# A three-layer transformer block in two stages: keys and values side by side, other PSUM banks, a stacked last chunk, gather first

## The reference

```
x = x + cross_attention(layernorm(x), context)   # 16 heads, 257 context rows, own context for each sequence
x = x + ssd(layernorm(x))                        # Mamba-2 with convolution, softplus(dt), cumulated decay, norm
x = x + moe(layernorm(x))                        # 8 experts, top 2, silu(z Wg) * (z Wu), Wd; inner width 704
```

## Time and profile before

| | us |
|---|---|
| median of 3 runs | 1529.26 |
| lowest, highest | 1528.14, 1529.80 |
| the profiled execution, whole | 1529.16 |
| its span | 1527.2 |
| stage one, full tiles | about 105 to 967 |
| tail of stage one and start of stage two | 967 to 1016 |
| stage two | 1016 to 1527 |

### The profile page before, as it was taken

One profiled execution on the slowest core, in us unless ns is written; L12 is line 12 of the kernel. 1 busy time (PEld: TensorE's weight loads), 2 busy tenths in 40 slices (PEclk: granted clock), 3 DMA queues, 4 the chain that ended last, 5 costly groups with the idle time before them and its releaser, 6 DMA issues.

```text
span 1527.2 us, 53971 instructions
## 1 busy us (share of the span) xinstructions
PE 1422.5 (93%) x15668; PEld 1294.9 (85%) x15669; DVE 1125.5 (74%) x3967; ACT 1000.9 (66%) x2482; POOL 838.1 (55%) x1401
## 2 busy tenths in 40 slices
PE   6969999999999999999999999649999999999997
PEld 5858888888888888888888888449999999999997
DVE  3647777777777777777777777557877787787775
ACT  4726766767766766766766676237777777677674
POOL 4514655655655655565565554226665666566554
PEclk9969999999999999999999999569999999999999
DMA  5302544554333343343343331425555555556554
GB/s 187 81 12 81 167 140 130 165 159 128 110 103 90 98 114 90 88 119 88 97 117 86 87 81 41 180 78 160 143 162 140 155 145 160 138 144 161 137 141 111
DMA packets 102009, 183.81 MB, mean 120 GB/s; under 512 B 19392, under 2 KB 61376, under 8 KB 101792
## 3 DMA queue, kind: packets, MB, share of 16 engines
q1 hardware_dynamic: 86272, 164.35, 35.2%
q0 software_dynamic: 15680, 18.76, 7.0%
HBM read 152.63 MB, written 31.13 MB: 120 GB/s over the span
## 4 chain that ended last, share of the span: by engine, by line
PE 72%; DVE 8%; issue 6%; ACT 2%; DMA 2%; POOL 1%; POOLq 1%; DVEq 0%; ACTq 0%; SPq 0%
PE m L412 12%; PE k L412 10%; PE y_p L1420 9%; PE v_p L412 9%; PE up_p L1420 8%; PE gate_p L1420 8%; PE sc L412 7%; PE pt L471 5%; PE ht_p L1459 3%; DVE dtv L976 2%; DMA par<-zbuf,gi 2%; ACT wd L735 1%; PE m L493 1%; PE z_p L1426 1%; DVE kT L868 1%
## 5 line engine op out<-in xcount | busy, mean ns | idle before, releaser
L735 ACT ACTIVATE wd<-wd,nmx 128x257 f32<-128x257 f32 x512 | 254.7, 499 | 100.6 <-DVE nmx L879 97.2
L879 DVE CUSTOM_DVE_ANT_0 wd<-sc,wd 128x257 f32<-128x257 f32 x512 | 187.3, 422 | 56.1 <-PE sc L412 45.8
L1622 POOL DMA_INDIRECT out<-par,oi x71 | 113.5, 1599 | 146.7 <-ACT par L1528 146.1
L1249 POOL TENSOR_TENSOR ctx_lo<-wd,ctx_hi 128x516 fp32r<-128x516 f32 x128 | 165.3, 1291 | 48.9 <-ACT ctx_hi L711 44.1
L711 ACT ACTIVATE wd<-pt 128x512 f32<-128x512 f32 x256 | 151.5, 592 | 57.9 <-PE pt L471 57.7
L471 PE MATMUL pt<-con,wd 128*128 128x128 f32 x1024 | 161.0, 280 | 3.0 <-ACT wd L735 0.7
L412 PE MATMUL k<-ctx_hi,wkh 128*128 128x256 f32 x512 | 158.2, 309 | 1.4 <-POOL ctx_lo L1249 1.4
L412 PE MATMUL v_p<-wvh,ctx_hi 128*128 128x256 f32 x512 | 158.0, 309 | 0.5 <-ACT y L711 0.5
L1499 ACT ACTIVATE uw_hi<-wu 128x1408 fp32r x71 | 98.3, 1385 | 85.1 <-PE up_p L1420 84.8
L1610 POOL COPY oi<-par 128x4 int32 x71 | 148.2, 2088 | 0.0
L1557 DVE TENSOR_TENSOR uw_lo<-wu,uw_hi 128x1408 fp32r<-128x1408 f32 x71 | 115.4, 1626 | 41.2 <-ACT uw_hi L1499 41.2
(11 more groups left out here) (197 smaller groups left out, 4662.2 us busy)
## 6 DMA issues: line engine op xcount, KB each, us to landing
dl<-d_low SPq DMA_DIRECT2D x71, 768.0 KB, 4.4
wd<-in_ctx SPq DMA_DIRECT2D x128, 258.0 KB, 2.8
wd<-in_mask SPq DMA_DIRECT2D x512, 32.1 KB, 1.8
wd<-in_wd SPq DMA_DIRECT2D x24, 256.0 KB, 3.0
d_high<-wd SPq DMA_DIRECT2D x24, 256.0 KB, 2.0
d_low<-wd SPq DMA_DIRECT2D x24, 256.0 KB, 2.3
wd<-d_high SPq DMA_DIRECT2D x8, 768.0 KB, 9.1
wg<-in_wg SPq DMA_DIRECT2D x8, 704.0 KB
```

What stands on the lines that cost most here:

```text
L735: nc.scalar.activation(pr[:, g, :], sm[:, g, :], ACT.Exp, bias=nmx[:, g:g + 1], scale=-1.0, accum_out=rsum[:, g:g + 1]).then_inc(exp_done, 1)
L879: V.tensor_tensor_reduce(sm[:, g, :], SC[g][:, 0:S], msk[:, b, :], -1.0, 3.0e38, ALU.add, ALU.min, nmx[:, g:g + 1]).then_inc(max_done, 1)
L1249: G.tensor_tensor(ctx_lo[:, b % 2], ctx[:, b], ctx_hi[:, b % 2].bitcast(F32), ALU.subtract).then_inc(lo_done, 1)
L1622: G.indirect_dma_start(outd[:, :], bass.IndirectOffsetOnAxis(oi[:, s, 1:2].bitcast(U32), 0), yb[:, s, :], None, compute_op=ALU.add).then_i ...
```

## The change

In stage one:
- TensorE's step becomes: scores of the next sequence, the side work that stood at the end of the step before (`turn_c`), keys and values of the one after the next, `turn_a`, weighted values, first transposes, `turn_b`, second transposes.
- Outputs and reciprocals go to the keys' bank, the second transposes to the values' bank. `px` gets two buffers.
- Softplus keeps its running sum and two helpers in a free part of the second score bank in PSUM; VectorE's steps of it stand between other operations, and the scores of sequence 1 of a tile wait for its last operation.
- The orders of ACT, VectorE and POOL are written anew: `keep`, `take_z2T`, `take_z3T`, `decays`, `residual1`, `statistics2`, `place`, `statistics1` and others stand in other places.

In stage two:
- The last chunk holds its 64 rows of h twice. The second half is turned into the low part, and its weights in DRAM are doubled by two more DMAs, so two matmuls do what three did.
- `turn_z` stands before `gate`, not behind it.
- POOL gathers three slots ahead, and first in its turn.

```diff
-                for c in range(FC):
-                    last = product(YB[:, 0:D], [h[:, c, :] for h in hT],
-                                   (wd[:, bass.ds(e, 1), c, :].rearrange("p o n -> p (o n)"), dl[:, s, c, :]),
-                                   c == 0, c == FC - 1)
+                for c in range(FC - 1):
+                    product(YB[:, 0:D], [h[:, c, :] for h in hT], weights(c), c == 0, False)
+                for k, w in enumerate(weights(FC - 1)):
+                    last = mm(YB[:, 0:D], hT[0][:, FC - 1, :], w, False, k == 1)
...
-                gate(t, s)
                 if not last:
                     turn_z(t + 1, 1 - s)
+                gate(t, s)
                 up(t, s)
...
+                V.tensor_tensor(hb[:, F:FC * P], sg[:, 1, FH - FL:FH], UB[:, 1, FH - FL:FH], ALU.mult).then_inc(h_done, 1)
...
-                low(flat(hT[1][:, 4:FC, :]), HB[1][:, 0:2 * P], flat(hT[0][:, 4:FC, :]), hT_done)
+                low(hT[1][:, 4, :], HB[1][:, 0:P], hT[0][:, 4, :], hT_done)
+                low(hT[0][FL:P, FC - 1, :], HB[1][FL:P, P:2 * P], hT[0][FL:P, FC - 1, :], hT_done)
...
+            for parts in (d_high, d_low):
+                last_chunk = parts.rearrange("p (e c d) -> p e c d", e=E, c=FC)[:, :, FC - 1, :]
+                sp.dma_start(last_chunk[FL:P], last_chunk[0:FL]).then_inc(twin_out, 16)
...
+        OT = K[:, 0:NH * 2 * Q].rearrange("p (a h q) -> p a h q", a=NH, h=2)
+        RP = K[0:2 * H, NH * 2 * Q:NH * 2 * Q + Q]
...
+                if b == 1 and runs(i - 2):
+                    pe.wait_ge(a_done, i - 1)
...
+                if d and runs(following(i, b)[0]):
+                    pe.wait_ge(v_done, n + 2)
...
+                if runs(following(i, b, 2)[0]):
+                    pe.wait_ge(k_done, 2 * n + 6)
...
-            su, sr, sy, sw, ss = dtv[:, 2, :], dtv[:, 3, :], dtv[:, 4, :], dtv[:, 8, :], dtv[:, 9, :]
+            su, sy, sw = dtv[:, 2, :], dtv[:, 4, :], dtv[:, 3, :]
+            sr, sp_y, sp_sum, ss = (SC[1][:, SP + k * H:SP + (k + 1) * H] for k in range(4))
```

## The result

| | us |
|---|---|
| predicted | 1521, range 1450 to 1545 |
| measured, median of 4 | 1541.71 (1541.27 to 1542.41) |
| before, on the same chip | 1528.70 (1527.59 to 1529.80) |
| ratio | 1.0086, 95% interval 1.0068 to 1.0103 |

The change makes the kernel 0.9% slower. The time lies in the range; the sign of the forecast was wrong. The span is 1539.8 us against 1527.2, 12.6 more. The first gate of stage two starts at 1004.95 instead of 1016.50, so stage one with its tail gives back 11.6 us (42 were forecast), and stage two takes 24.2 more (34 were forecast).

What follows compares the result with a forecast made beforehand. TensorE was taken to bound both stages, with a POOL, ACT and VectorE loop nearly as long in stage two. Stage one -42 us and stage two +34 us took 1529.16 to 1521 us, range 1450 to 1545.

Steps and rivals of the forecast that it cites:

- start-up saved, keys and values adjacent: Stage one, TensorE: fp32r start-up after fp32 matmuls paid once a batch less, 0.32 us a tile saved, bounds 0.2 and 0.45.
- `ynT`, early transposes: Stage one: transposes of y a values projection earlier, exponentials given 1.5 us more; 0.45 of 0.53 us a tile saved.
- softplus: Stage one: VectorE's last softplus operation about 0.4 us earlier, so `sum_a`'s wait of 0.47 us a tile goes.
- the jump: End of TensorE's loop body in stage one: four early transposes hide 0.36 of 0.56 us a tile, bounds 0 and 0.56.
- new waits: Stage one, outputs and second transposes in other banks: 0.20 us a tile of added TensorE waits, bounds 0 and 0.6.
- fill idle time; a step later, each is still ahead of its reader: Stage one: moved `keep`, `place` and statistics stay within their engines and cost nothing.
- Stage two: POOL, ACT and VectorE loop lengthens slots from 6.87 to 7.6 us; +34 us in all, from +27 to +41.
- B: Rival, stage two: the `oi` copy slips in ahead of `uw_lo`, TensorE sets slots of 6.67 us; 1461 us, chance 0.22.
- the held state: Stage two: `uw_lo` blocks POOL's `oi` copy, ACT's copy of y waits, slots of 7.6 us; the state sustains itself.
- C: Rival: the held state, and stage one's scores wait for the last softplus operation; 1548 us, chance 0.15.
- D: Rival, stage one: PSUM operands make twelve softplus operations 0.065 us longer each, 18 us in 30 tiles; 1539 us, chance 0.05.
- A: Main forecast, both stages: stage one -42 us, stage two +34 us; 1521 us, own range 1503 to 1540, chance 0.58.

Runs made afterwards that it cites:

- o_place_series: Changed kernel with POOL's `oi` copy ahead of the gather, `place` moved to step 1, first three softplus pieces behind both keys copies: 1488.9 us (0.970).
- before_two: Kernel before the change, with TensorE's loop running two tiles a turn and nothing else: 1522.0 us (0.995).
- o_place_two: Changed kernel with POOL's `oi` copy ahead of the gather, `place` moved to step 1, TensorE's loop over two tiles a turn: 1481.4 us (0.968).
- o_place: Changed kernel with POOL's `oi` copy ahead of the gather and VectorE's `place` moved from step 2 to step 1: 1486.8 us (0.968).

## Why the prediction was right and wrong, step by step

| term, us a tile of stage one | in the sum | measured | from |
|---|---|---|---|
| start-up saved, keys and values adjacent | -0.32 | -0.36 | values 1.50 to 1.41 in each of four batches |
| `ynT`, early transposes | -0.45 | -0.40 | start to start: 0.29 to 0.15 and 0.76 to 0.50 |
| softplus | -0.47 | -0.64 | row gone (it returns in `o_place_series`); 0.47 idle, 0.64 start to start |
| the jump | -0.36 | -0.19 | `before_two`, `o_place_two` |
| new waits | +0.20 | +0.96 | 0.41 (`o_place`) + 0.27 + 0.28 |
| sum | -1.40 | -0.63 | tile: -0.64 on the mean |

What `sum_a` cost before is read from three rows of the kernel before and from 419.82 in the earlier trace rows: `sum_a` starts 1.07 us behind the transposes of 418.75, and where nothing waits the next matmul starts 0.43 behind the same four transposes.

```profile
412.66 0.60 PE L471 MATMUL pt<-con,wd 128*128 128x128 f32 x4
413.09 0.38 PE L493 MATMUL m<-con,z 128*128 128x128 f32 x2
...
418.75 0.60 PE L471 MATMUL pt<-con,wd 128*128 128x128 f32 x4
```

**The step that failed is "I take nothing for them alone and put 0.2 us a tile of new waits into the sum, bounds 0 and 0.6."** The new waits are 0.96. Three things were missed in it. First, 0.41 of it comes from an edit that I set at nothing ("fill idle time; a step later, each is still ahead of its reader"): `place`, 1.2 us of small operations, stands ahead of the queries' scaling, and its cost falls on what is queued behind it, not on its own reader. `o_place` shows it. Second, the softplus pieces between maxima and keys were counted as cover for softplus, not as a delay of the keys: that is the 0.27 at 415.71, which `o_place_series` takes away. Third, the values' copy was said to be ready 0.2 us early in the last step and is 0.28 late: ACT starts it only when the weighted values are done. That is read from ACT's timeline and from the start of 417.25, no run took it away alone:

```profile
416.50 0.60 ACT L720 ACTIVATE wd<-v_p 128x512 f32<-128x512 f32 x1 [1.16 <-PE k L418]
```

With softplus at 0.64 the terms add up to the tile, and nothing of size is left over. The four gains were forecast at 1.60 and came to 1.59, but by luck: softplus gave 0.17 more than forecast and the jump 0.17 less.

**The jump** was mis-sized: it was taken at 0.36 and is 0.19. The edit hides 0.19 of its 0.50, not most of it.

**Outside the loop** I put 7 us of gain for the five unrolled tiles and the first two. By the starts of the `yn` transposes the two full tiles ahead of the loop are 0.9 us shorter together and the three behind it as long as before, so 0.9 came of 7. And the start is slower: the first `yn` transposes stand 5.48 us later than before (117.45 against 111.97). 4.96 of it is there already at the first matmul of the state-space output (93.45 against 88.49), ahead of these transposes. What was lost there no run looked for; the cause is open. Together: 4.6 us behind at the head of the loop, 15.2 gained in the 24 tiles measured inside it, about 1 more by the tiles and the tail behind it, which makes the 11.6.

**The bounds.** The lower end of stage one, -18 us, does not follow from the bounds of its parts. At their bad ends these make a tile 0.2 us longer (0.2 + 0.2 + 0 + 0 - 0.6), 6 us slower over 30 tiles, so the measured -11.6 lay within them and outside the range that was drawn from them.

**Stage two** was right in its mechanism, its trigger and its price. The term that was off is the length of the slot, 7.38 instead of 7.6 with bounds 7.5 and 7.7: `gw_lo` starts at Y+2.65, not at Y+2.92 as in the earlier trace rows, since ACT, late with y, has h ready at once and goes on to `gw_hi` sooner. All that hangs on it moves by 0.27. The sum then is 64 x 0.51 = 33, less 12 for late gathers, one late gather of 1.9 left and the ends: +24. The stacked chunk gave its 0.12 us a slot, the z transposes ahead of `gate` 0.01 instead of 0.08 (6.87 - 0.119 = 6.75, and the slot is 6.74).

**The rivals.** B, the copy ahead of `uw_lo`, never came up: the held state began in the first slots and never let go, as argued. C (1548) did not happen: the scores wait for no softplus operation, and its 0.47 went. What it had right is only that VectorE would hold TensorE somewhere in the tile. D (1539) did not happen either: the operations last the same with PSUM and SBUF operands (0.17 and 0.18 us), and one of them in SBUF alone costs 1.2 us more, for another reason. Both times are nearer to 1541.7 than A's 1521, and that is luck. A's own range ended at 1540; the whole range took the result in by 3 us, and only because the slot of stage two was shorter than forecast, which gave back 10 of the 30 us that stage one missed.

Had the new waits been put at 0.96, a tile would have come to -0.64, the loop to -16 us, with the 7 outside it to -23, and the total to 1529 - 23 + 34 = 1540: a forecast of slower. The bounds of the term, not only its value, were too narrow, since they looked at the edited waits alone and not at what stands behind the moved operations.

## What to carry to other kernels

When steps are put in another order, price each moved operation on the queue behind it: the next one with a reader on the bounding engine can pay for it (`place`, 1.2 us long, cost 0.41 us a tile). A tiny copy on POOL that someone waits for must not stand where a long VectorE operation of two SBUF tensors can start ahead of it; put it earlier, or cut the long one in pieces, and both brought the slot from 7.38 to 6.74 us here. Edits that look separable (an order and a bank) may be worth a gain together and a large loss alone, so try each by itself before a verdict on either.

## What the runs showed that was not expected

- A PSUM operand can be worth far more than its own latency: it keeps a VectorE operation out of the exclusion with POOL. One operation of 16 columns went from 0.17 to 1.34 us without it, and the kernel from a ratio of 0.977 to one of 1.026 (with the scores' wait for softplus taken out in the same run).
- The exclusion acts both ways: POOL's copy of four columns ended only with `gw_lo` (2.16 us in its row, about 0.6 of it behind the scatter), and VectorE's operation waited as long as POOL's subtraction lasted.
- Stage two has two steady rhythms, 6.74 and 7.38 us a slot, 45 us over 70 slots, in programs that differ by the place of one call on POOL, or by one VectorE instruction cut in four.
- TensorE waited 0.4 us in each slot of the held state with the granted clock at 1.00 throughout, while one wait of 1.47 us in a tile was followed by 0.65 and 0.80.
